# Two layer norms around the second attention, moved into its batch loop

## The reference

```python
x = x + _L0_ffn_ref(_layernorm(x), ...)      # 16 experts, one for each row, and a shared expert
x = x + _L1_xattn_ref(_layernorm(x), ctx_1024, ctx_1024, ...)   # 16 heads of 16, with Wq, Wk, Wv, Wo and biases
x = x + _L1_ffn_ref(_layernorm(x), ...)      # 8 experts, each takes its best 64 rows of a batch
```

## Time and profile before

| | |
|---|---|
| median of 3 runs | 1626.47 us (1623.16 to 1627.51) |
| the profiled execution | 1631.14 us, its span 1629.4 us |
| PE busy | 1458.9 us (90%) |
| DVE busy | 942.6 us (58%) |
| ACT busy | 874.4 us (54%) |
| POOL busy | 638.8 us (39%) |
| second attention, first to last step of DVE | 1020.7 to 1268.3 us |
| fourth stage, DVE's first step to the first of the fifth stage | 1269.1 to 1299.3 us |

### The profile page before, as it was taken

How to read it: one execution, slowest core, us unless ns; L and a number is a source line. 1 busy time by engine, 2 the same in 40 slices (tenths; PEclk the granted TensorE clock), 3 DMA queues, 4 the chain that set the end, 5 groups by cost and what they waited for, 6 DMA issues and landing times. The chain is left out here.

```text
span 1629.4 us, 28395 instructions
## 1 busy us (share of the span) xinstructions
PE 1458.9 (90%) x9884; PEld 1193.4 (73%) x9884; DVE 942.6 (58%) x1777; ACT 874.4 (54%) x2184; POOL 638.8 (39%) x886
## 2 busy tenths in 40 slices
PE   4999999999999999877999994799998539999995
PEld 4878887878787888666888883466564528888885
DVE  5776767666767676655311116577877554444442
ACT  3886868677868686624211113566664214444442
POOL 6514444434444430323200015332231025787875
PEclk9999999999999999988999997899999559999998
DMA  4400000000000000012699963000000313455442
GB/s 137 164 1 21 1 21 2 21 3 20 2 14 8 1 1 1 1 33 83 220 314 312 317 210 52 26 8 14 8 1 1 127 61 110 124 121 123 120 123 27
DMA packets 74448, 120.27 MB, mean 74 GB/s; under 512 B 7008, under 2 KB 55136, under 8 KB 74304
## 3 DMA queue, kind: packets, MB, share of 16 engines
q1 hardware_dynamic: 63600, 101.76, 19.4%
q0 software_dynamic: 10704, 16.65, 5.1%
HBM read 99.78 MB, written 18.61 MB: 73 GB/s over the span
## 5 line engine op out<-in xcount | busy, mean ns | idle before, releaser
L508 ACT ACTIVATE a_p<-a_s,a_negmax 128x512 f32<-128x512 f32 x256 | 176.2, 688 | 111.6 <-DVE a_negmax L632 61.4
L632 DVE TENSOR_REDUCE a_negmax<-a_s 128x1 f32<-128x512 f32 x256 | 176.5, 689 | 76.6 <-PE a_s L371 72.7
L273 POOL TENSOR_TENSOR a_o_l<-a_o,a_o_h 128x256 fp32r<-128x256 f32 x64 | 46.9, 735 | 299.5 <-ACT a_o_h L533 299.5
L1561 ACT ACTIVATE h_probs<-h_scores,h_negmax 128x256 f32<-128x256 f32 x256 | 118.0, 475 | 81.7 <-DVE h_negmax L1728 81.7
L380 PEld LDWEIGHTS a_t<-ident,a_p 128*128 128x128 f32 x1024 | 122.5, 141 | 51.3 <-issue 21.6
L380 PE MATMUL a_t<-ident,a_p 128*128 128x128 f32 x1024 | 157.1, 276 | 0.7 <-DVE a_pT L647 0.7
L1973 POOL TENSOR_TENSOR n_w_l<-n_raw,n_w_h 128x768 fp32r<-128x768 f32 x64 | 118.2, 1847 | 75.3 <-ACT n_w_h L2016 75.3
L398 PE MATMUL a_out_p<-a_pT,a_v 128*64 128x256 f32 x1024 | 124.6, 385 | 0.0
L370 PE MATMUL a_s<-a_k_hl,a_q_hh 128*128 128x512 f32 x256 | 106.4, 415 | 2.6 <-issue 1.9
L1728 DVE TENSOR_REDUCE h_negmax<-h_scores 128x4 f32<-128x1024 f32 x64 | 78.0, 1221 | 49.4 <-PE h_scores L1655 49.4
L1666 PEld LDWEIGHTS h_turned<-ident,h_probs 128*128 128x128 f32 x512 | 54.7, 141 | 64.7 <-issue 45.8
(11 more groups left out here) (357 smaller groups left out, 4382.1 us busy)
## 6 DMA issues: line engine op xcount, KB each, us to landing
e_w_in<-in_L_ffn_gate_up_proj SPq DMA_DIRECT2D x31, 1024.0 KB, 7.1
n_raw<-in_L_ffn_w SPq DMA_DIRECT2D x64, 384.0 KB, 3.1
e_w_out<-in_L_ffn_down_proj SPq DMA_DIRECT2D x31, 512.0 KB, 5.4
rows_in<-a_zeros SPq DMA_DIRECT2D x1, 3968.0 KB, 15.3
e_rows<-rows_in SPq DMA_DIRECT2D x31, 128.0 KB, 5.3
rows_out<-e_result POOLq DMA_DIRECT2D x31, 128.0 KB, 4.6
a_both<-in_ctx SPq DMA_DIRECT2D x8, 256.0 KB, 2.7
a_both<-in_x SPq DMA_DIRECT2D x8, 256.0 KB, 3.0
```

Source lines behind the costliest of these rows:

```text
L508: act.activation(probs[j][:, :], scores[j % 2][:, :], ACT.Exp, bias=negmax[:, j:j + 1], accum_out=total[:, r % 2, j % 2, j // 2:j // 2 + 1 ...
L632: dve.tensor_reduce(negmax[:, j:j + 1], scores[j % 2][:, :], AX.X, ALU.max, negate=True).then_inc(max_set, 1)
L1561: ins = act.activation(probs[s % 4][:, j, :], scores[s % 2][:, j // 2, j % 2, :], ACT.Exp, bias=negmax[:, s % 4, j:j + 1], accum_out=total ...
```

## The change

It leaves the arithmetic of the result as it is up to rounding, and moves both norms.

- **Mixture.** POOL gathers only the tiles 0 to 7 here. Only batches 0 and 1 are normalised and turned: DVE runs `normalise(0)` before its part of step n = 15, ACT applies it before its part, PE turns both batches before the last `down`, and `add` of the last group is DVE's last instruction. In the steps 0 to 11 `add` goes ahead of the pieces of routing, and the pieces are spread over n = 3, 4, 5 and 6, one each.
- **Second attention, before.** DVE normalises batches 2 and 3 at the start of the stage (`normalise_first`). For batches 4 to 7 POOL does it: `gather(b)` (two indirect DMAs), `centre(b)` (sum by halving, mean, subtract, square) and `scale(b)` (sum by halving, root, multiply). In iteration b, batch b+4 is centred and scaled and batch b+5 gathered. PE transposes batch b+2 after s = 3 into `proj` (`turn_x`), ACT takes the high part (`high_x`), DVE the low part (`low_x`); `project_q(b+1)` moves from s = 3 to s = 2, and `project_out` waits for `low_x`.
- **Second attention, after.** At s = 7 DVE measures batch b-1 (`measure`), and at the end of iteration b POOL normalises batch b-2 into `xn` (`keep`). The last two are done after the loop, batch 6 on POOL and batch 7 on DVE (`keep_last`). SP stores `x` and `xn` batch by batch.
- **Fourth stage.** `find_gates` only turns `xn`, copies and multiplies with the gate; the logits of all batches lie in one PSUM tile and are copied once.

```diff
@@ run_mixture: POOL, PE, ACT, DVE
-                for t in range(NT):
-                    if t < TILES * EARLY:
-                        pool.wait_ge(added, t // TILES + 1)
+                for t in range(2 * TILES):
+                    pool.wait_ge(added, t // TILES + 1)
                     pool.indirect_dma_start(g.x[:, t, :], None, g.rows_out[:, :],
...
-                for b in range(NB):
+                for b in range(2):
                     turn_sums(b)
+                down(FC * GROUPS - 1)
...
                 for n in range(FC * EARLY, FC * GROUPS):
+                    if n == FC * GROUPS - 1:
+                        apply(0)
+                        apply(1)
                     silu_of(n)
                     high_of(n)
...
                     shared(n)
-                    if n == 3:
-                        route(1)
-                    elif n == 4:
-                        route(2)
-                        route(3)
-                    elif n == 5:
-                        route(4)
+                    if n % FC == 0 and n:
+                        add(n // FC - 1)
+                    if n in range(3, 7):
+                        route(n - 2)
                     elif n == 8:
                         scale_queries()
-                    if n % FC == 0 and n:
-                        add(n // FC - 1)
...
+                    if n == FC * GROUPS - 1:
+                        normalise(0)
                     shared(n)
...
-                normalise(0)
-                normalise(1)
-                for b in range(NB):
+                for b in range(2):
                     low_x(b)
...
+                add(GROUPS - 1)
@@ attend_context: POOL
                 low_ctx(1)
+                gather(LATER)
                 for b in range(NB):
...
                         low_o(b - 1, 1)
+                    if b + LATER < NB:
+                        centre(b + LATER)
                     add_bias(b)
                     spread_inverse(b, 0)
+                    if b + LATER < NB:
+                        scale(b + LATER)
                     if b + 2 < NB:
                         low_ctx(b + 2)
                     low_o(b, 0)
+                    if b + LATER + 1 < NB:
+                        gather(b + LATER + 1)
+                    if b >= 2:
+                        keep(b - 2)
                 spread_inverse(NB - 1, 1)
                 low_o(NB - 1, 1)
+                keep(NB - 2)
@@ attend_context: PE
                 def project_out(b):
                     pe.wait_ge(ol_set, KC * b + KC)
-                    if b + 2 < NB:
+                    if b + 1 + FIRST < NB:
+                        pe.wait_ge(xl_set, b + 2)
+                    elif b + 2 < NB:
                         pe.wait_ge(q_set, b + 3)
...
-                        if s == 3 and b + 1 < NB:
+                        if s == 2 and b + 1 < NB:
                             project_q(b + 1)
+                        if s == 3 and b + FIRST < NB:
+                            turn_x(b + FIRST)
@@ attend_context: DVE
+                        if s == 4 and b + FIRST < NB:
+                            low_x(b + FIRST)
...
+                        if s == 7 and b:
+                            measure(b - 1).then_inc(measured, 1)
...
                 add(NB - 1)
+                keep_last()
```

More of the change, by code:

```diff
@@ L1468, in _, with store @@
             def _(sp):
+                out_rows = io["out"].rearrange("b (t p) d -> p b t d", p=P)
+                def store(b):
+                    sp.wait_ge(added, b + 1)
+                    sp.dma_start(out_rows[:, b, :, :], g.x[:, 2 * b:2 * b + 2, :]).then_inc(stored, 16)
+                    sp.wait_ge(kept, b + 1)
+                    sp.dma_start(xn_rows[:, b, :, :], g.xn[:, 2 * b:2 * b + 2, :]).then_inc(stored, 16)
                 for b in range(NB):
@@ L1471, in _ @@
                     sp.dma_start(ctx_raw[:, :, :], ctx_dram[:, :, b * S:(b + 1) * S]).then_inc(ctx_in, 16)
+                    if b >= 4:
+                        store(b - 4)
+                for b in range(NB - 4, NB):
+                    store(b)
+                sp.wait_ge(stored, 32 * NB)
             @block.gpsimd
@@ L1810, in _, with turn, find @@
                 sp.dma_start(gate[:, :, :], io["L1_ffn_gate_w_T"].rearrange("(c p) e -> p c e", p=P)).then_inc(gate_in, 16)
-                sp.dma_start(io["out"].rearrange("b (t p) d -> p (b t) d", p=P), g.x[:, :, :]).then_inc(stored, 16)
+            @block.tensor
+            def _(pe):
+                def turn(b):
+                    wait(pe, filled[b % 2], b // 2)
+                    for kc in range(KC):
+                        for t in range(2):
+                            ins = pe.transpose(turned_ps[b % 2][:, kc, t * P:(t + 1) * P],
+                                               g.xn[:, 2 * b + t, kc * P:(kc + 1) * P], g.ident[:, :])
+                    ins.then_inc(turned, 1)
+                def find(b):
+                    pe.wait_ge(filled[b % 2], b // 2 + 1)
+                    for t in range(2):
+                        for kc in range(KC):
+                            ins = pe.matmul(logit_ps[:, t, b, :], full[b % 2][:, kc, t * P:(t + 1) * P],
+                                            gate[:, kc, :], start=(kc == 0), stop=(kc == KC - 1))
+                    ins.then_inc(logit_done, 1)
+                turn(0)
+                turn(1)
+                pe.wait_ge(gate_in, 16)
@@ L1857, in _ @@
+                for b in range(0, NB, 2):
+                    act.wait_ge(turned, b + 1)
+                    wait(act, logit_done, b - 1)
+                    act.activation(full[0][:, :, :], turned_ps[0][:, :, :], ACT.Copy).then_inc(filled[0], 1)
             @block.vector
             def _(dve):
-                link = Chain(dve, norm.chain)
-                def fill(b, par):
+                for b in range(1, NB, 2):
+                    dve.wait_ge(turned, b + 1)
                     wait(dve, logit_done, b - 1)
-                    norm.fill(dve, b, par)
@@ L1866, in step @@
-                def step(b, par, first, last):
-                    wait(dve, kept, b - 1)
-                    norm.apply(dve, b, par)
-                    if not first:
-                        fill(b - 1, 1 - par)
-                norm.moments(dve, link)
-                batches(dve, NB, step)
-                fill(NB - 1, 1)
+                    dve.tensor_copy(full[1][:, :, :], turned_ps[1][:, :, :]).then_inc(filled[1], 1)
+                dve.wait_ge(logit_done, NB)
+                dve.tensor_copy(g.logits2[:, :, :, :], logit_ps[:, :, :, :]).then_inc(logit_set, 1)
@@ L2232, in program @@
             clear_semaphores(nc)
[L2233 to L2237 removed]
+            find_gates(nc, g, io)
             clear_semaphores(nc)
```

283 lines of the change are left out of this document (149 added, 134 removed).

## The result

| | before | after |
|---|---|---|
| median of 4 executions | 1626.99 us | 1648.47 us |
| ratio after / before | | 1.012, interval 1.0084 to 1.0155 |
| profiled execution (span) | 1631.14 us (1629.4) | 1645.91 us (1644.2) |
| PE busy | 1458.9 us | 1470.3 us |
| POOL busy | 638.8 us | 716.0 us |

A forecast was written before the change was run, and what follows sets the result against it. PE's own order was taken as the second attention's bound, with POOL as free room. Terms -6 - 20.4 + 30.2 + 1.5 - 1.7 = +3.6 us gave a median of 1630.1 us, own range 1623 to 1637, 8 in 10 within 1616 to 1643.

The forecast's parts named there:

- Entry, -6 (bounds -2 and -9): Entry to the experts: `add` ahead of routing removes PE's 5.54 us wait, rows loaded earlier; 6 us less.
- the entry gains nothing: Rival at the experts' entry: reordering only trades PE's wait for one on the rows; +6, 1636 us; chance 0.07.
- End of the mixture, -20.4: From `normalise(0)` to POOL's first step of the next stage: ends at 999.9 instead of 1020.4; bounds -18.5 and -21.
- The order on PE, +9.7: Attention loop: query projection ahead of the scores of s = 3 adds 1.4 us in iterations 0 to 5, 1.3 in 6.
- `measure`, +5.7: Attention loop: 0.95 us on DVE ahead of the copy PE awaits at each batch's start, batches 2 to 7.
- The copies, +6.2 and +8.6: Attention loop: PE waits for POOL's inverses, 6.2 us by `centre` before the first, 8.6 by `scale`, gather, `keep` before the second.
- the rival of POOL's stretched steps: Slower rival in the attention loop: POOL's chains 15% longer, PE waits more; +12, 1642 us; chance 0.19.
- The clock, +1.5 (0 to 4): Attention loop: a PE wait of 4 us also brings the granted clock down; +1.5 us, between 0 and 4.
- The gates, -1.7: Gate stage, last addition to choice: 29.3 us instead of 31.0, PE still the bound at 2.43 us a batch; bounds 0 and -3.
- The rival, a clock that rises there: Gate stage: the clock rises since all transposes come early with nothing between; -8, 1622 us; chance 0.06.

The follow-up runs named there:

- The edit alone: Kernel before with only `add` ahead of the routing and one piece of routing a step; 1626.2 us, ratio 0.9997.
- POOL's wait: POOL's four subtractions wait for the third `add`, on the kernel after and on the kernel before with reordered routing; the latter 1624.1 us, ratio 0.9969.
- three moves: Kernel after with `measure` at s = 6, `keep` where POOL idled, only the mean ahead of the first copy; clock never fell; 1624.4 us, ratio 0.9976.
- second execution of the same loop: Kernel after with one edit in the mixture and none in the attention loop; loop 251.1 us against 258.1, 1636.3 us in one run.
- six waits of 2.2 us: Kernel before with nine dependent POOL steps ahead of the first copy of the inverses in iterations 1 to 6; 1640.2 us in one run.
- `measure` moved: Kernel after with `measure` behind `add` at s = 6 instead of at s = 7; 1646.8 us, ratio 1.0119.
- `keep` moved: Kernel after with `keep` in iterations 4 to 7 where POOL idled, stores behind all loads of ctx; 1642.6 us, ratio 1.0084.
- `centre` split: Kernel after with only the halving for the mean ahead of the first copy of the inverses; 1649.2 us, ratio 1.0125.

## Why the prediction was wrong

**Entry, -6 (bounds -2 and -9).** -5.3 in the two traces, but by luck: the trace of before was the slowest of four with the old order (88.0, 85.0, 85.7 and 82.4 us from the first attention's last addition to the first turn), and nine with the new order have 82.7 to 85.2. The edit alone gave 0.9997. The rival "the entry gains nothing" was right, with another wait than it named: not the rows, but DVE held up beside POOL. The forecast took POOL to be out of the way there once the scatters were issued; its four subtractions had moved next to DVE's last step. The scatters and the issue of the loads came where they were forecast (53.7 and 76.9 us behind that addition, against 53.6 and 77.0; the sum's 774.1 should read 773.9, which changes nothing). The first load then needed 2.1 us and not 4.1: with POOL's wait the first turn comes after 78.7 us, where 81.2 was said.

**End of the mixture, -20.4.** 24.85 instead of 45.44 us from the first gather on: -20.6. `normalise(0)` began at 977.85, 9.6 us behind the first gather, as worked out. The start of the stage was taken as unchanged and is 1.2 us longer, by the load of ctx.

**The order on PE, +9.7.** A batch of the iterations without any new wait but `measure` is 31.1 us; less 0.95 that is 1.45 over 28.70, where 1.4 was said.

**`measure`, +5.7.** The wait went from 0.74 to 1.69 us at the start of six batches, 5.7: right. At s = 6 the wait was 0.74 again.

**The copies, +6.2 and +8.6.** 1.93 + 1.89 + 1.88 = 5.7 (none in iteration 0), and 2.25 + 3.98 = 6.2, where 4.1 + 0.4 + 4.1 stood. The chain itself was right: from the end of the first copy to the end of the second in iteration 2 it is 20.1 us, where 20.4 was said. PE, though, was ready for `weigh` only 17.8 us behind the first one and not 16.3, by the low stretch at 1104: 1.5 us of the clock's cost lie hidden in the shorter wait. POOL's times carried over from the first attention to 0.1 us; the rival of POOL's stretched steps did not come.

**The clock, +1.5 (0 to 4).** This is the step that failed. It was sized by one wait of 4 us. There were eleven waits of 1.7 us or more at the full clock, and seven low stretches; the same matmuls were busy 16.3 us longer than in the kernel without a fall. What the other terms leave for it is 13.4 us (41.3 less 27.9), and 6.4 in the second execution of the same loop: against the forecast's 1.5, in both cases outside its bounds. The six waits of 2.2 us show that no fixed price for a wait would have done: the forecast needed a range for this term that reached well past its 4. The other terms of the loop sum up to 27.9, against 30.2. Why the clock falls behind one wait and not behind the next stays open.

**The gates, -1.7.** -0.4: `keep_last` and its store stand ahead of PE, 9.8 us without a matmul, and then PE needs its 2.45 us a batch at the slow level as forecast, with the gate's load beside its first transposes. What was too small is `keep_last`, 5.9 us instead of 4.75. One of its small steps, said to be 0.2 us, took 1.00:

```profile
1284.83 1.00 DVE L1807 TENSOR_SCALAR h_z_guess<-h_z_var 128x2 int32<-128x2 int32 x1
```

Why it did so is not shown. The rival, a clock that rises there, did not come: 0.50 over 15 us in which the profile shows PE busy without a gap. The Trainium skill, page "TensorE: Matmul & The Clock Gate" (What's actually happening), gives an array that has been busy its full clock. This row disagrees with it, as the one of before did, if busy means there what it means in the profile.

**The rest of the 19.4 us**, 4.6, is the place of the two profiled executions among those of the same code. How much one can differ from the next shows at the start of the attention stage: the clock was back at 1.00 within 4 us in the kernel after and with three moves, within 12 with `measure` moved, and after 23 with `keep` moved, with `centre` split and in the second execution of the changed loop. The first `weigh` then came 26.4, 29.3 and 32.8 to 33.1 us behind the first projection. None of these edits touches what PE does or waits for in that stretch.

## What to carry to other kernels

On an engine that bounds a stage, add up the new waits first, and then ask for the clock: here 17.6 us of new waits came with another 13.4 us of lower clock in one execution and 6.4 in another, so the term needs a wide range. Small steps are free only in a slot where their engine idles and nothing behind them is awaited: the same `measure` cost 0.95 us a batch at s = 7 and nothing at s = 6, the same `keep` 6 us or nothing. Taking work from one stage into another pays only if the stage it leaves was bound by it: the gate stage lost only 0.4 us until what remained ran beside PE, and then 7.

## What the runs showed of the hardware

- A DVE instruction with two SBUF inputs took 5.39 us instead of 0.69 beside four POOL instructions of the same kind, and 3.02 beside two of them.
- The granted clock fell behind some waits and not behind others of the same length: 7 of 11 in the kernel after, 1 of 6 waits of 2.2 us in the probe. The same loop, with the same waits, took 258.1 us in one execution and 251.1 in another.
- At the start of the attention stage the same code got its full clock back after 4 to 23 us, and its first `weigh` came 26.4 to 33.1 us behind the first projection.
